# Moving the compares of a top-307 threshold search from VectorE to ScalarE in a sparse-attention and channel-mix kernel

## What is computed

```python
q, k, v = (split_heads(x @ W + b) for W, b in ((Wq, bq), (Wk, bk), (Wv, bv)))
scores = einsum('bhqd,bhkd->bhqk', q, k) * 0.25          # 4096 x 4096 for each of 32 heads
sparsity = scores.max(-1) - scores.mean(-1)
_, top_idx = top_k(sparsity, 307)                        # U = 307 queries of each head
attn = softmax(q[top_idx] @ k.T * 0.25) @ v              # only for these
out = zeros_like(q).at[top_idx].set(attn)
x = layernorm(x + out @ Wo + bo)
r, k2 = sigmoid(mix_r(x) @ W_r), square(relu(mix_k(x) @ W_k))
x = layernorm(x + r * (k2 @ W_v))
```

## Time and profile before

| | |
|---|---|
| median of 3 runs | 3516.61 us (3513.26 to 3524.34) |
| the profiled execution | 3517.38 us, of which the span that the trace covers is 3515.6 us |
| mean granted TensorE clock | 0.968 of full speed |
| busy share of the span | PE 88%, DVE 86%, ACT 79%, POOL 42% |
| first and last `main` on ScalarE | 81.7 and 3177.5 us |
| the tail (last search, rest of attention, feed of batch 1) | from about 3180 us |

### The profile page before, as it was taken

The page is one execution under the profiler, slowest core; times in us unless marked ns, Lnnn a source line. Parts: engine busy times, 40 slices in busy tenths (PEclk is TensorE's granted clock), DMA queues, the critical chain, the costliest instruction groups (busy, mean ns, idle before and its releaser), DMA issues.

```text
span 3515.6 us, 58457 instructions
## 1 busy us (share of the span) xinstructions
PE 3093.8 (88%) x15873; PEld 1429.4 (41%) x15873; DVE 3018.9 (86%) x6367; ACT 2784.8 (79%) x5893; POOL 1491.2 (42%) x2606
## 2 busy tenths in 40 slices
PE   5999999997799998898999868899988898897688
PEld 3334333342244433433444434544444443344466
DVE  3889988899989899899898769888998789986478
ACT  3889888897789998798899746699966598894555
POOL 2210022100136633453555435666545653448754
PEclk8999999999999999999999989999999999998799
DMA  6422232326121251141122141112151123113022
GB/s 185 147 81 36 62 86 74 83 37 9 24 44 32 38 32 32 32 32 31 32 38 38 37 32 41 42 35 38 32 44 41 34 42 15 30 20 15 14 76 70
DMA packets 262291, 163.60 MB, mean 47 GB/s; under 512 B 167563, under 2 KB 241483, under 8 KB 257867
## 3 DMA queue, kind: packets, MB, share of 16 engines
q1 hardware_dynamic: 255819, 158.50, 25.7%
q0 software_dynamic: 6144, 1.37, 0.5%
HBM read 111.86 MB, written 47.86 MB: 45 GB/s over the span
## 4 chain that ended last, share of the span: by engine, by line
PE 31%; DVE 24%; ACT 19%; issue 19%; POOL 3%; SPq 2%; DMA 1%; ACTq 0%; DVEq 0%; POOLq 0%
ACT AB L846 15%; DVE JK L985 13%; PE CP L580 10%; PE DP L584 9%; ACT E L867 4%; DVE msk L1020 3%; PE PV L691 2%; PE PV L692 2%; PE BP L676 2%; DVE SPr L985 1%; DVE fst L1131 1%; PE PV L528 1%; PE BP L528 1%; DVE VF L1169 1%; PE BP L714 1%
## 5 line engine op out<-in xcount | busy, mean ns | idle before, releaser
L985 DVE CUSTOM_DVE_ANT_0 JK<-DP,AB 128x1024 bf16<-128x1024 f32 x2048 | 2467.7, 1221 | 321.8 <-ACT AB L846 103.1
L846 ACT ACTIVATE AB<-CP 128x512 f32<-128x512 f32 x4096 | 2228.5, 598 | 402.6 <-PE CP L580 341.2
L580 PE MATMUL CP<-KS,QS 128*128 128x512 f16 x4096 | 1393.6, 387 | 67.2 <-issue 16.2
L584 PE MATMUL DP<-KS,QS 128*128 128x512 f16 x4096 | 1239.9, 385 | 120.2 <-DVE SPr L985 102.1
L1353 POOL TENSOR_TENSOR SCR<-E 128x307 f16<-128x307 f32 x967 | 671.8, 707 | 564.2 <-ACT E L867 557.1
L580 PEld LDWEIGHTS CP<-KS,QS 128*128 128x128 f16 x4096 | 393.3, 97 | 793.9 <-ACT AB L846 659.0
L584 PEld LDWEIGHTS DP<-KS,QS 128*128 128x128 f16 x4096 | 343.9, 98 | 515.7 <-DVE SPr L985 330.3
L867 ACT ACTIVATE E<-BP 128x307 f32<-128x307 f32 x882 | 384.7, 436 | 54.8 <-PE BP L676 49.5
L1213 POOL TENSOR_SCALAR SCR<-SCR 128x48 f16<-128x48 f16 (+2 forms) x122 | 49.7, 407 | 564.7 <-DVE SCR L953 321.6
L676 PE MATMUL BP<-QT,KA 128*128 128x307 f16 x882 | 261.8, 297 | 19.6 <-ACT QT L859 17.5
L691 PE MATMUL PV<-E,XT 128*128 128x307 bf16 x512 | 163.1, 319 | 30.8 <-POOL SCR L1353 30.5
(11 more groups left out here) (352 smaller groups left out, 2818.3 us busy)
## 6 DMA issues: line engine op xcount, KB each, us to landing
KS<-KTC SPq DMA_DIRECT2D x256, 128.0 KB, 4.9
QS<-QSC SPq DMA_DIRECT2D x512, 64.0 KB, 2.2
KA<-KTC SPq DMA_DIRECT2D x128, 128.0 KB, 3.9
QN<-SCR SPq DMA_DIRECT2D x16, 544.0 KB, 3.4
SCR<-in_L_attn_x SPq DMA_DIRECT2D x16, 512.0 KB, 6.7
KTC<-SCR SPq DMA_DIRECT2D x32, 256.0 KB, 2.2
QSC<-SCR SPq DMA_DIRECT2D x32, 256.0 KB, 2.4
AO<-E SPq DMA_DIRECT2D x2, 4096.0 KB, 22.0
```

What stands on the lines that cost most here:

```text
L580: pe.matmul(o, qs, ks[j][:, 1, :], start=True, stop=True).then_inc(sc_c, 1)
L584: r = pe.matmul(o[:, 512 * j:512 * j + 512], qs, ks[j][:, 0, :], start=True, stop=True)
L846: act.activation(AB[p % 3][:, 512 * j:512 * j + 512], BANK["C%d" % j], ACT.Abs).then_inc(ab_full, 1)
L985: dve.tensor_tensor_reduce(out=JK[p % 2][:], in0=BANK["D%d" % u], in1=AB[p % 3][:], scale=1.0, scalar=-3.0e38, op0=ALU.add, op1=ALU.max, a ...
```

## The change

The compares of groups 0 to 5 become ScalarE activations: `Sign(limit - value)` with the accumulator output gives (values below) minus (values above) for each partition, and a limit has its 307 when the sum over the head is at most 4096 - 614. For that the bits are split in integer halves, `HI` (upper 16 bits) and `LO`, by two VectorE instructions (`parts`); the first eight digits test `HI`, and then one more instruction puts `LO` less the distance to the found upper half into `ST` for the last eight. `digit` counts how many limits are met, and since limits are in steps of one size, the next ones are a multiply and an add, one sum of which is made ahead (`ahead_of`). Counts and the matrix `same` of `cnt` go from bf16 to f32. Group 6 keeps its compares on VectorE (`on` is "D"), in the new number format. The writes of the maxima to `QN` are issued head by head, one head with the first compare of a digit, and in the tail `gath` of a head follows `arr` of the head before.

```diff
     def select(g):
         n = GROUPS[g][2]
         gaps = 0 if tail[0] else 1
-        yield [("sel", g)]
-        for _ in range(3 * gaps):
-            yield []
+        on = "D" if tail[0] else "A"
         yield [("flip", g, bank())]
         for _ in range(gaps):
+            yield []
+        yield [("parts", g)]
+        for _ in range(2 * gaps):
             yield []
         for i, (_, w) in enumerate(DIGITS):
             if gaps:
                 for j in range(w):
-                    yield [("cmp", g, i, j)]
+                    yield [("cmp", g, i, j, on)] + ([("sel", g, i)] if j == 0 and i < n else [])
+            else:
+                yield [("cmp", g, i, j, on) for j in range(w)] + ([("sel", g, i)] if i < n else [])
+            bk = bank()
+            yield [("cnt", g, i, bk), ("digit", g, i, on, bk)]
+            for _ in range(gaps):
                 yield []
-            else:
-                yield [("cmp", g, i, j) for j in range(w)]
-            bk = bank()
-            yield [("cnt", g, i, bk), ("digit", g, i, bk)]
-        for _ in range(3 * gaps):
+        for _ in range(2 * gaps):
             yield []
         yield [("cut", g, bank())]
...
         yield [("ka", 0), ("qgzero",)] if g == 0 else []
-        for h in range(n):
-            yield [("gath", g, h)]
+        yield [("gath", g, 0)]
         for _ in range(5 * gaps):
             yield []
         for h in range(n):
-            yield [("arr", g, h)]
+            yield [("arr", g, h)] + ([("gath", g, h + 1)] if h + 1 < n else [])
...
+            def cmp(g, i, j, on):
+                if on == "A":
...
+                    if i == 0 or i == LOW:
+                        act.wait_ge(sel_key, 2 * g + (1 if i == 0 else 2))
+                    if j == 0 and i:
+                        act.wait_ge(sel_lim, 16 * g + i)
...
+                    r = act.activation(hits[j][0:rows, :], (HI if i < LOW else ST)[0:rows, :], ACT.Sign, scale=-1.0,
+                                       bias=limits_of(i)[0:rows, j + 1:j + 2], accum_out=cnt3[0:rows, j:j + 1])
...
+            def parts(g):
+                rows = 16 * GROUPS[g][2]
+                dve.wait_ge(sel_st, g + 1)
+                after(dve, sel_f, g)
+                bits = ST[0:rows, :].bitcast(I32)
+                dve.tensor_scalar(HI[0:rows, :], bits, 16, 16, ALU.arith_shift_right, ALU.logical_shift_left)
+                dve.tensor_scalar(LO[0:rows, :], bits, 65535, None, ALU.bitwise_and).then_inc(sel_key, 1)
...
+                if plain:
+                    dve.tensor_scalar(ahead_of[0:rows, :], steps[0:rows, i + 1, :], now[0:rows, 0:1], None, ALU.add)
                 dve.wait_ge(sel_pe, SEL0[g] + 2 + i)
...
+                q = seq.mark(dve.tensor_scalar(met[0:rows, 0:w], BANK[bank][0:rows, 0:w], goal, None, how, ALU.add,
+                                               accum_out=met[0:rows, 3:4]))
+                dve.wait_ge(q_dve, q)
+                count = met[0:rows, 3:4]
+                if plain:
+                    dve.scalar_tensor_tensor(out=new[0:rows, :], in0=count.broadcast_to([rows, 4]), scalar=step,
+                                             in1=ahead_of[0:rows, :], op0=ALU.mult, op1=ALU.add).then_inc(sel_lim, 1)
+                    return
...
-            def sel(g):
+            def sel(g, h):
                 b, h0, n = GROUPS[g]
-                sp.wait_ge(l_q, 128 * (b + 1))
-                sp.wait_ge(cap, g + 1)
-                for h in range(n):
-                    c0 = (h0 + h) * (DH + 1) + DH
-                    for u in range(2):
...
```

More of the change, by code:

```diff
@@ L379, in attention_rwkv @@
         msk3 = sb("msk3", [128, NT, 8], BF16)
-        cnt3 = sb("cnt3", [128, 4], BF16)
-        same = sb("same", [128, 8, 16], BF16)
-        steps = sb("steps", [128, len(DIGITS), 3], I32)
-        test = sb("test", [128, 4], I32)
-        best = sb("best", [128, 2, 4])
+        cnt3 = sb("cnt3", [128, 4])
+        same = sb("same", [128, 8, 16])
+        steps = sb("steps", [128, len(DIGITS), 4])
+        limit0 = sb("limit0", [128, 4])
+        limit8 = sb("limit8", [128, 4])
+        test = sb("test", [128, 2, 4])
+        ahead_of = sb("ahead_of", [128, 4])
+        met = sb("met", [128, 4])
+        upper = sb("upper", [128, 1])
+        best = sb("best", [128, 2])
         need = sb("need", [128, 8])
@@ new lines, in cmp @@
+            def cmp(g, i, j, on):
+                if on == "D":
+                    rows, w = 16 * GROUPS[g][2], DIGITS[i][1]
+                    if (i, j) == (0, 0):
+                        dve.wait_ge(consts, 2)
+                        after(dve, sel_m, 5 * g)
+                    if i == 0 or i == LOW:
+                        dve.wait_ge(sel_key, 2 * g + (1 if i == 0 else 2))
+                    if j == 0 and i:
+                        dve.wait_ge(sel_lim, 16 * g + i)
+                    if j == 0:
+                        after(dve, sel_pe, SEL0[g] + 1 + i if i else 0)
+                    r = dve.tensor_scalar(hits[j][0:rows, :], (HI if i < LOW else ST)[0:rows, :],
+                                          limits_of(i)[0:rows, j + 1:j + 2], None, ALU.is_ge, ALU.add,
+                                          accum_out=cnt3[0:rows, j:j + 1])
+                    if j + 1 == w:
+                        r.then_inc(sel_cmp, 1)
```

96 lines of the change are left out of this document (55 added, 41 removed).

## The result

The changed kernel takes 3494.11 us, median of 4 runs (3488.91 to 3497.93), against 3517.22 of before on the same chip: ratio 0.9931, 95% interval 0.9909 to 0.9953, 23 us less. A second measurement with more runs gave 0.9949 (0.9935 to 0.9962). The time lies inside the range, but the gain is less than half of the 50 us forecast. The profiled execution took 3497.08 us with a span of 3495.3, 20.3 less than that of before.

The account below looks back on a forecast made before the run. VectorE, which runs the compares, was taken to set the pace in five searches of seven or nearly so; -17 + 0 - 18 - 22 + 5 + 2 = -50 gave 3466 us, range 3436 to 3498 for 8 in 10.

Parts of the forecast that it names:

- The writes of the maxima, -22: At group 3, the 24.2 us wait for feed tile 6 behind ten writes goes, 2 us left for later lateness: -22 us.
- rival C: The stall at group 3 moves to feed tile 7, half of 22 us comes back: 3480 us, chance 0.12.
- Price of a compare, 0.49: One compare on ScalarE costs 0.49 us, against 0.40 on VectorE; bounds 0.36 and 0.60.
- rival B: ScalarE is the new bound, as a compare there costs 0.60 us: 3497 us, chance 0.13.
- Group 0, -17: In the search of group 0 a digit takes 6.4 us in place of 7.46, for 16 digits -17 us.
- Groups 1, 2 and 5, 0: Searches beside attention: VectorE is freed, ScalarE filled, a digit 7.43 us against 7.46 before, sum 0.
- Groups 3 and 4, -18: Searches beside the feed: gain between 0 and 18 us a group, 9 taken for each, -18 us.
- Waits that come in: ScalarE's wait for new limits fits by 0.2 us; the count on TensorE has no wait left behind the third compare.
- rival E: Limits reach ScalarE too late, each digit loses 1.15 us: slower than before, 3576 us, chance 0.06.
- The tail, +2: Tail: digits +2, gathers in turn +4, two attention steps fewer -2, L1038 less exposed -2; together +2 us.
- Small parts, +5: Splitting into halves, the subtraction and last joins add about 1.3 us of VectorE a search, exposed in groups 0, 3, 4: +5.
- rival F: Sign needs another activation table, two loads of 1.283 us for each of 276 compares: over 700 us, chance 0.02.

Follow-up runs that it names:

- e16: The changed kernel with six more main steps between the index write and the first gather in groups 0, 3 and 4: ratio 0.9862, 3469.4 us.
- e6: The changed kernel with all compares on VectorE and the empty main step of a digit put back ahead of the count: ratio 0.9974, 3509.9 us.
- e7: The changed kernel, compares on ScalarE, with an empty main step ahead of the count as well as the one behind the digit: ratio 0.9916.
- e1: The kernel before with only the writes of the maxima spread, one head per digit, every compare still on VectorE: ratio 0.9905.
- e9: The kernel before with only the spread writes of the maxima, compares on VectorE, measured once more on another occasion: ratio 0.9910.

## Why the prediction was wrong, step by step

- **The writes of the maxima, -22.** Right in mechanism and somewhat small: about 24 to 28 us in the search of group 3, 0.9% (some 32 us) alone. No wait over 10 us is left there, rival C didn't happen.
- **Price of a compare, 0.49.** Right to the hundredth, so rival B as put (0.60) is out. Yet the whole came out near B's 3497, for other reasons.
- **Group 0, -17.** The step that failed is "so 1.06 less than 7.46, for 16 digits". It summed each engine over a digit and took the larger. The steps have different limits, and three buffers of absolute values don't level them: 6.66, so 0.80 less. And it took all 16 digits as equal: the first four still lie beside the values, where nothing is won. Measured -7.2.
- **The hand-over behind group 0, not in the sum.** This is the largest term that the prediction had at nothing without a reason: from row maximum 592 to 835 the kernel takes 358.9 us for 346.9, +12.0. 5.7 of it are the wait for the gather, whose index write had come to stand behind sixteen loads; 4.1 went with a stretch of 17.1 us at the lower clock, of which e16 has almost none.
- **Groups 1, 2 and 5, 0.** Measured +1.4, +2.4 and +1.3. ScalarE was full as forecast; the digit is 7.6 to 7.7 for 7.43.
- **Groups 3 and 4, -18.** The step that failed is "I take 9 each", the middle between 0 and 18. Group 4 has 138.4 against 138.5, and group 3 has 137.9 against 137.8 and 141.7 for the writes alone; by the clocks above it may be 2. The relief itself is there, 6.7 and 5.4 us against e6. What the prediction left out is that the new form and its plan cost about as much beside the feed, in part with a lower clock. VectorE was busy for 92% of group 4's search before, and nothing is above 86% now; what sets the pace there, no run isolates.
- **The f32 count, about +0.3 each on TensorE.** Can't be told from 0.
- **Waits that come in.** ScalarE waited for limits 1.7 us in all, twice: rival E is out, and the margin of 0.2 held. That the count "has no wait left" was wrong: TensorE sat idle 26.6 us in 48 places ahead of it, though e7 shows these harmless. The place of the empty step, which the prediction never priced, is worth 1.3% on VectorE; on ScalarE no run has it ahead alone.
- **The tail, +2.** 337.4 (3515.6 - 3178.2) became 340.9: +3.5. The gathers cost about what was said, the digits got no longer. By the rule on shared access ("SBUF — State Buffer" of the Trainium skill, "Who interferes with whom") the new multiply-add, with two inputs in SBUF, would be held up as L1038 was. The trace agrees: the median of L1075 is 0.159 us, and the longest took 3.08 us, from 3186.96 on, while six low halves of GpSimd (L1411) ran one behind the other.
- **Small parts, +5.** Too small: e6 shows that the new form with its plan costs some 20 us on VectorE, 11 of them in the hand-over behind group 0.
- **The table load, rival F.** Out, as a compare took 0.49. The product at the end of its paragraph comes to about 1.5 ms, not 1.4.

In the searches and the tail -7.2 + 5.1 - 27.5 - 0.1 + 3.5 are -26.2, the spans differ by 20.3; the 6 us between lie outside the searches, where +12.0 behind group 0 meet gains of some 6 elsewhere.

That the time fell inside the range is partly luck: the digit of group 0, the relief beside the feed and the hand-over all came out worse than forecast, and the writes of the maxima better.

## What to carry to other kernels

Price a move between engines step by step, with the slower engine of each step, and not by the totals of a stretch; and price what the move brings with it (here a new number format and a shifted plan), which beside the feed cost as much as the move gained. Follow a shortened stage to its hand-over: if the next stage waits for a transfer that doesn't get shorter, or for an in-order queue that such a transfer blocks, the gain ends there, and a few steps of other work put in between can bring more than the stage itself. In a plan written by hand, an empty step ahead of an in-order engine's wait is part of the design (1.3% here, with the compares on VectorE), so a diff that moves one is not neutral. Before a difference of a few us between two traces is read as an effect of the code, compare the granted clock of the stretch.

## What the hardware showed that I had not expected

- A small write to memory issued directly behind sixteen loads on the same queue let its read follow after 5.9 us, one issued 3 us behind them after 1.4; over all traces 5.0 to 6.4 us against 1.2 to 2.8.
- Counts on TensorE in f32 (two matmuls) gave 0.993 to 0.995, in bf16 (one) 0.993: 96 more matmuls at 0.2 us cost nothing measurable.
- Two profiled executions of one program (e1 and e9) differ by 7.9 us in span, 4 of them in the search of group 3 (141.7 and 137.8), where the granted clock was 0.94 and 0.98: beside the feed a single trace tells nothing smaller.
